# An attention kernel of eight batches: roundings of keys one unit later on ScalarE, values moved out of the key gaps, and a fifth buffer of probabilities

## What is computed

```python
x = x + _L0_xattn_ref(_layernorm(x), ctx, ...)   # q, k with rotary positions, scores + temporal bias, softmax, gate
x = x + _L0_ffn_ref(_layernorm(x), ...)          # three matrices and tanh
x = x + _L1_xattn_ref(_layernorm(x), ctx, ctx, mask, ...)
x = x + _L1_ffn_ref(_layernorm(x), ...)          # 8 experts, the best 2 weighted
# within an attention, per head:
scores = jnp.einsum('bhqd,bhkd->bhqk', q, k) * SCALE
attn = jax.nn.softmax(scores, axis=-1)
out = jnp.einsum('bhqk,bhkd->bhqd', attn, v)
```

## Time and profile before

| | before |
|---|---|
| median of 3 runs | 566.13 us (564.79 to 567.99) |
| the profiled execution | 565.75 us, its span 564.2 us |
| TensorE busy | 508.7 us (90%) |
| ScalarE busy | 434.1 us (77%) |
| VectorE, GpSimd busy | 278.4 and 168.3 us |
| exponentials, 416 in all | 1.03 us each |
| batch 0, 1, 2 end about at | 119, 187, 255 us |
| batches 4 to 7 | 54 to 56 us each |

### The profile page before, as it was taken

One profiled execution on the slowest core, in us unless ns is written; L12 is line 12 of the kernel. 1 busy time (PEld: TensorE's weight loads), 2 busy tenths in 40 slices (PEclk: granted clock), 3 DMA queues, 4 the chain that ended last, 5 costly groups with the idle time before them and its releaser, 6 DMA issues.

```text
span 564.2 us, 15361 instructions
## 1 busy us (share of the span) xinstructions
PE 508.7 (90%) x6338; PEld 260.1 (46%) x6338; DVE 278.4 (49%) x739; ACT 434.1 (77%) x496; POOL 168.3 (30%) x202
## 2 busy tenths in 40 slices
PE   7779898989889898899999999999999999998995
PEld 4434545445345544454555444444443443443344
DVE  5866556864785446553523252326343623450254
ACT  1265577777668787887988999899989988999832
POOL 4476817485685306840001001100000000000000
PEclk9788999999999999999999999999999999999996
DMA  8586965398568513671464383149112920000000
GB/s 270 157 264 207 292 214 151 130 291 264 131 189 271 168 43 95 220 231 52 96 146 146 95 167 93 60 106 230 57 37 69 222 75 7 7 1 2 6 6 16
DMA packets 51584, 74.53 MB, mean 132 GB/s; under 512 B 11146, under 2 KB 40050, under 8 KB 51506
## 3 DMA queue, kind: packets, MB, share of 16 engines
q1 hardware_dynamic: 40258, 37.54, 26.4%
q0 software_dynamic: 5632, 24.07, 12.7%
q10 hardware_dynamic: 5616, 11.86, 6.6%
HBM read 39.95 MB, written 18.83 MB: 104 GB/s over the span
## 4 chain that ended last, share of the span: by engine, by line
PE 59%; ACT 14%; issue 10%; DVE 8%; POOL 5%; DMA 3%; ACTq 1%; DVEq 0%
PE ps L539 26%; PE ps L515 16%; ACT probs L1167 9%; PE ps L450 3%; PE ps L440 2%; PE ps L669 2%; ACT ctx_turned L1167 1%; DVE k_swapped L1476 1%; PE ps L444 1%; ACT ctx_tokens L1167 1%; DMA k_scratch<-k_parts 1%; ACT k_parts L1192 1%; PE ps L551 1%; ACT ctx_normed L1167 1%; DMA wvg_columns<-in_wvg_columns 1%
## 5 line engine op out<-in xcount | busy, mean ns | idle before, releaser
L1167 ACT ACTIVATE probs<-ps 124x1024 f32<-124x1024 f32 (+1 forms) x305 | 296.3, 1025 | 53.1 <-PE ps L520 41.7
L515 PE MATMUL ps<-q_side,k_side 64*124 64x256 bf16 (+1 forms) x1664 | 162.0, 290 | 35.3 <-ACT probs L1167 26.6
L539 PE MATMUL ps<-probs,values 124*9 124x256 f32 (+1 forms) x2440 | 162.8, 382 | 0.0
L515 PEld LDWEIGHTS ps<-q_side,k_side 64*124 64x124 bf16 (+1 forms) x1664 | 79.6, 131 | 142.0 <-ACT probs L1167 74.7
L539 PEld LDWEIGHTS ps<-probs,values 124*9 124x9 f32 (+1 forms) x2440 | 52.8, 90 | 64.6 <-issue 17.4
L1051 POOL TENSOR_TENSOR post_rstd<-post_rstd,power 128x2 f32<-128x2 f32 x12 | 8.5, 712 | 194.0 <-DVE post_rstd L1691 126.5
L520 PE MATMUL ps<-bias_near,bias_w 64*124 64x84 bf16 (+1 forms) x416 | 42.2, 200 | 0.0
L1167 ACT ACTIVATE ctx_tokens<-ps 124x1024 f32<-124x1024 f32 (+1 forms) x37 | 38.0, 1026 | 5.0 <-PE ps L515 4.0
L1476 DVE SCALAR_TENSOR_TENSOR k_swapped<-ps,beta_products,k_table_sb 32x496 f32<-32x496 f32 (+2 forms) x64 | 40.4, 632 | 0.9
L1167 ACT ACTIVATE ctx_turned<-ps 124x1024 f32<-124x1024 f32 (+1 forms) x37 | 37.9, 1025 | 3.4 <-PE ps L515 2.4
L1167 ACT ACTIVATE ctx_normed<-ps 124x1024 f32<-124x1024 f32 (+1 forms) x37 | 37.9, 1026 | 2.4 <-PE ps L515 1.6
(11 more groups left out here) (256 smaller groups left out, 633.3 us busy)
## 6 DMA issues: line engine op xcount, KB each, us to landing
k_side<-k_scratch SPq DMA_DIRECT2D x24, 400.2 KB, 8.1
k_scratch<-k_parts POOLq DMA_DIRECT2D x16, 372.0 KB, 4.9
k_side<-k_parts SPq DMA_DIRECT2D x45, 124.0 KB, 2.4
q_side<-q_parts SPq DMA_DIRECT2D x63, 64.0 KB, 2.4
v_scratch<-values POOLq DMA_DIRECT2D x4, 936.0 KB, 8.8
values<-v_scratch SPq DMA_DIRECT2D x4, 936.0 KB, 13.9
v_scratch<-v POOLq DMA_DIRECT2D x12, 288.0 KB, 5.0
mask_q<-in_mask POOLq DMA_DIRECT2D x8, 400.5 KB, 4.5
```

What stands on the lines that cost most here:

```text
L515: last = pe.matmul(ps[0:width, bank, SQ * i:SQ * (i + 1)], kst[rows, j % 2, 2 * g + i, at], qst[rows, query_slot(j, run), 2 * g + i, :], s ...
L539: last = pe.matmul(ps[32 * i:32 * i + VC, ACC + g // 2, SQ * (g % 2):SQ * (g % 2) + SQ], v[0:rows, j % 2, t, h, :], probs_of(u)[0:rows, SQ ...
L1167: act.activation(probs_of(u)[0:rows, :], ps[0:rows, s:s + 2, :].rearrange("p a n -> p (a n)"), ACT.Exp)\
```

## The change

Six things are changed. ScalarE's roundings of layer 1's keys come 3 and 7 units behind the key step, where it was 2 and 6. In batches 1 and 2 `values_at` gives no unit of values in the pair whose even slot begins a key step, and four in the pair after it. For that to be possible in batch 2, its steps move from slots 7, 11, 18, 25 to 8, 12, 18, 26. There is a fifth buffer of probabilities, used from batch 1 on (so eight buffers from batch 3 on). The memory for it comes from `num` and `q_table`, which now lie in it; both are used only in batch 0. And `store_keys(0, 0)` is split: the stores of the keys go before `second_parts(1)`, that of the values stays behind it.

```diff
-        first = {at: (j + 1, n) for n, at in enumerate((10, 14, 20, 26) if j == 1 else (7, 11, 18, 25))}
+        first = {at: (j + 1, n) for n, at in enumerate((10, 14, 20, 26) if j == 1 else (8, 12, 18, 26))}
...
     if j < WIDE_FROM:
-        return 2
+        key_pairs = [] if j == 0 else [at // 2 for at in range(2 * VALUES_FULL) if keys_at(j, at) is not None and keys_at(j, at)[2] == 0]
+        return 0 if pair in key_pairs else 4 if pair - 1 in key_pairs else 2
...
-            return u % 4 if u < WIDE_FROM * UB else (u - WIDE_FROM * UB) % 7
+            return u % 4 if u < UB else (u - UB) % 5 if u < WIDE_FROM * UB else (u - WIDE_FROM * UB) % 8
...
-        num, den, inside = sb("num", [128, SQ]), sb("den", [128, SQ]), sb("inside", [128, SQ], BF16)
+        num, den, inside = p_fifth[:, 2 * SQ:3 * SQ], sb("den", [128, SQ]), sb("inside", [128, SQ], BF16)
...
             low_parts(1)
+            store_keys(0, 0, "k")
             second_parts(1)
-            store_keys(0, 0)
+            store_keys(0, 0, "v")
...
-                for lag, part in ((2, second_keys), (6, middle_of_second)):
+                for lag, part in ((3, second_keys), (7, middle_of_second)):
```

More of the change, by code:

```diff
@@ L190, in main_path @@
         near = sb("bias_near", [128, KT, NEAR], BF16)
[L191 removed]
+        p, p_fifth = sb("probs", [128, 4, HG * SQ]), sb("probs_fifth", [128, HG * SQ])
         def prob_slot(u):
[L195 removed]
+            return u % 4 if u < UB else (u - UB) % 5 if u < WIDE_FROM * UB else (u - WIDE_FROM * UB) % 8
         def probs_of(u):
             slot = prob_slot(u)
[L200 removed]
+            return p[:, slot, :] if slot < 4 else (p_fifth[:], ct[:], cn[:], tok[:].rearrange("p t d -> p (t d)"))[slot - 4][:, 0:HG * SQ]
         def taken_ahead(u):
@@ L246, in main_path @@
         rab = sb("x_rstd", [128, XT, 2])
-        q_table = sb("q_table_sb", [128, 2, SQ])
+        q_table = p_fifth[:, 0:2 * SQ].rearrange("p (i n) -> p i n", n=SQ)
         q_cos, q_sin = q_table[:, 0, :], q_table[:, 1, :]
@@ L1271, in scalar_program @@
             act.dma_start(G["centre_ident"][:], G["centre_ident_in"]).then_inc(ident_in, 16)
-            act.dma_start(q_table[:], G["q_table"]).then_inc(q_tab_in, 16)
+            act.dma_start(q_table, G["q_table"]).then_inc(q_tab_in, 16)
             act.dma_start(wvg_columns[:], G["wvg_columns"]).then_inc(beta_in, 16)
```

34 lines of the change are left out of this document (18 added, 16 removed).

## The result

| | before | after |
|---|---|---|
| median | 565.46 us (4 runs, 563.68 to 567.99) | 560.0 us (4 runs, 558.98 to 560.27) |
| ratio, with its interval | | 0.990 (0.9877 to 0.9923) |
| the profiled execution, its span | 565.75 us, 564.2 us | 560.2 us, 558.6 us |
| first exponential of the loop starts | 29.87 us | 31.09 us |
| TensorE's idle time before score matmuls in 58 to 255 us, nearly all of it for exponentials | 15.3 us | 5.6 us |

The account below looks back on a forecast made before the run. TensorE, waiting for ScalarE's exponentials, was taken as the bound. Head 3.7, rest of batch 0 1.33, batch 1 0.92, batch 2 2.0, narrow steps -0.1 sum to 7.85 us: forecast 558.3 us, range 551.5 to 563.

Parts of the forecast that it names:

- What bounds the kernel: Batches making keys, 58 to 255 us: TensorE's 15.3 us of score waits for ScalarE's exponentials fall to about 6.
- The later roundings: Key-step gaps: the second exponential runs in ScalarE's 1.19 us of idleness; costs nothing, removes TensorE's 1.14 us wait.
- The sum for batch 2: Batch 2's four gaps: 0 for the first two, 0.9 for the third, 0.65 + 0.44 for the last; 2.0 us.
- No values in the gap, four units after it: Batches 1 and 2: same matmuls in another order, values covering ScalarE's rounding and next two exponentials; no cost outside narrow steps.
- the narrow step: Chunk 0, 124 keys: 0.4 us lost in batch 1, 0.3 won in batch 0; together -0.1, between -0.9 and +0.8.
- Batch 1: Gaps of batch 1: the first ones worth 0 because VectorE and GpSimd limit them; only the last gap's 0.92 us kept.
- The 1.14 us: Batch 1, before chunk 2's keys: the time won turns into TensorE waiting for VectorE, worth 0.
- The head: Start of batch 0: loop starts 1.1 to 1.4 us later, stall and slow stretch go; 3.7 us won, bounds 1.9 to 5.1.
- VectorE's chain moves up by 1.9 us: Batch 0's head: token load ends at 47.7, so k_swapped of chunk 3 comes 1.9 us earlier; 2.4 taken for TensorE's matmuls.
- The second term, 1.3: Batch 0's head: TensorE's 1.32 us wait at 60.60 goes, as ScalarE has one more exponential before it waits for GpSimd.
- the clock takes the head: Rival: idle before unit 2 and before 55 us drops the clock again, costing about the head's 3.7; 562 us, chance 0.15.
- Slower, by the middle rounding: Rival: GpSimd's L1029 waits for the later middle rounding, lengthening nine wide chunks, 9.2 us less 3.7; 571.6 us, chance 0.05.

Follow-up runs that it names:

- experiment 1: Kernel before with one edit: ScalarE's roundings of layer 1's keys 3 and 7 units behind the key step; ratio 0.993 to the kernel before.
- experiment 9: Kernel before with lags of 3 and 7 and batch 2's key steps at even slots 8, 12, 18, 26; 559.7 us, ratio 0.990.
- experiment 7: Changed kernel with two units of values in every pair of batches 1 and 2 again; 557.37 us, ratio 0.986 to the kernel before.
- experiment 4: Changed kernel with the roundings' lags back at 2 and 6; ratio 1.011 to the kernel before.
- experiment 2: Kernel before with lags of 3 and 7 and the stores of chunk 0's keys moved ahead of the second roundings; ratio 0.994.
- experiment 3: Changed kernel with the stores of chunk 0's keys back behind the second roundings of chunk 1; 558.85 us, ratio 0.989 to the kernel before.
- experiment 5: Changed kernel with the next batch's token load issued behind unit 2 instead of unit 6; 557.14 us, ratio 0.986 to the kernel before.
- experiment 6: Changed kernel with the middle rounding 6 units behind the key step instead of 7; 555.69 us, ratio 0.983 to the kernel before.
- experiment 10: Changed kernel with the token load behind unit 2 and the middle rounding 6 units behind; 558.67 us, ratio 0.988 to the kernel before.
- experiment 8: Changed kernel with matmuls on zeros in two of TensorE's waits in batch 0's head; 559.24 us, ratio 0.990 to the kernel before.
- experiment 11: Changed kernel with early token load, middle rounding at 6 and the stores of chunk 0's keys back as before; 559.03 us, ratio 0.986.
- experiment 12: Changed kernel with early token load, middle rounding at 6, stores as before and two units of values everywhere; 558.23 us, ratio 0.987.

## Why the prediction was right, and which step was mis-sized

*What bounds the kernel.* Right: TensorE's idle time before score matmuls in the three batches went from 15.3 to 5.6 us (about 6 was forecast), and the gaps kept what the chain behind them allowed.

*The later roundings.* Right as a mechanism, and it is the edit that carries the change in batches 0 and 1 (1.9 and 1.0 us with the lag alone). Wrong that it costs nothing wherever the step stands: with the odd slots of batch 2 it lost 1.4 us there, most of it at the lower clock behind a wait that had grown by 0.4 us. I had taken the new slots of batch 2 as a condition for the order of the values. They are a condition for the lag, worth 4.2 us (experiments 1 and 9). The sum for batch 2 came out right because both were in the change.

*No values in the gap, four units after it.* I took it as neutral but for the narrow step. It costs 0.6 us in batch 2 (experiments 7 and 9 against the changed kernel), within the bounds given for the narrow steps. What I did not see is that without the lag batches 1 and 2 lose 11.8 us with it, 5.4 of them to the lower clock (experiment 4).

*Batch 1.* The 1.14 us did turn into a wait for VectorE: 2.06 us until 148.41. The 0.92 us came out at 0.98. It is not safe, though: in experiments 1, 2, 3, 5, 6, 7 and 10 TensorE stood 0.6 to 1.2 us at the batch's end for the load of the far queries, and experiments 2, 3 and 5 kept 0.1, 0.1 and -0.1 us of it. The sum had no term for the clock here either, and the wait for VectorE brought a slow stretch (148.9 us). TensorE's waits for v and k_swapped from 58 to 255 us grew by 3.7 us, from 2.1 to 5.8, a little less than the 4 to 5 that were forecast.

*The head.* Here the sum failed: 3.7 forecast, 1.08 measured. The start was 1.22 us later, as reckoned (GpSimd's second rounding of chunk 1 began at 29.21 instead of 27.88, behind the two stores), and the stall went. The failing step is "VectorE's chain moves up by 1.9 us". It rests on the load of the tokens ending at 47.7. I said that its issue hangs on unit 6, whose scores come no earlier, and left out that with a start 1.2 us later the issue also comes later: 39.9, not 38.8. And I took its 8.9 us for a fixed price. The runs show 7.6 to 12.7 us for this load issued at 38.8 to 40.0. The row statistics moved up by 0.46 us, and the matmuls behind k_swapped, which had stood 0.69 us in their queue, by 1.15, where the sum had 2.4. The second term, 1.3, was right: at the full clock the stretch behind them takes 3.80 us (experiment 8), and it took 5.32 before, 1.52 more. And the sum had no term for the clock, which took 1.58 of it back: 1.15 + 1.52 - 1.58 = 1.09, against 1.08 measured.

*The clock.* The rival "the clock takes the head", with a chance of 0.15, was in good part what happened, and at the places that it named: 1.66 us of idle before unit 2 and 2.71 before 56.60, each followed by a slow stretch. The sign that the prediction named for it, a clock of 0.50 between 28 and 60 us, was met. Only the second stretch cost the head anything, 1.6 us. The rival left nothing of the head where the execution kept 1.1, so 562 was too high and 558.3 too low; 560.0 lies between the two and in the range. The gaps gave 5.1 us where the sum had 4.15, and so covered a part of what the head fell short; that is luck and not reckoning.

*Slower, by the middle rounding.* Did not occur: in a wide chunk GpSimd's last difference of layer 1's keys waited for nothing.

```profile
148.76 1.13 POOL L1031 TENSOR_TENSOR k_parts<-k,k_parts 128x496 bf16<-128x496 f32 x1
```

That the middle rounding should have been moved the other way in relation to the next chunk, I had in hand: the prediction names the 2.91 us that GpSimd waits for it, and that it comes right behind the next chunk's first rounding. I used it to limit the gain and didn't see that one unit less would free it.

*What stays open.* The head's share in the medians is read from one trace per kernel and from the mean clock of the other executions. Whether the clock alone holds experiments 10 to 12 back in those was not seen in a trace. What brings the clock down in one execution and not in another is open too. A kernel with a lag of 6 everywhere but in chunk 3 of batch 0, and with the early load, should have both gains; it was not run.

## What to carry to other kernels

An instruction put later on an engine must be judged by what it then stands in front of: here the same lag took away a wait of 0.9 us behind an even slot and made one 0.4 us longer behind an odd one, and the same rounding freed GpSimd's chain when it moved past another rounding and stopped TensorE when it stood before an exponential. A wait that grows by 0.4 us can cost more than 0.4 if TensorE's clock falls behind it, so read the granted clock beside every wait. Where a stall goes, look at what is late next and whether its duration is a price or a draw: a load in a crowded stretch is a draw, so issue it before the crowd. And of a change with many parts, run the parts: two of six carried this one, and the order of the values made it slower than before when the later lag was taken away.

## What the runs showed of the hardware

The same load of the tokens took 4.5 to 6.4 us when it was issued at 31.3 to 34.0 us, and 7.6 to 12.7 us when it was issued at 38.8 to 40.0, with the DMA engines' share at 1.03 to 1.07 over 40 to 44 us in the changed kernel. The Trainium skill (DMA: Bandwidth & Descriptors, Queues, rings and completion order) says that each DMA engine takes turns between the queue rows that have work, packet by packet; a load that is longer when others are under way agrees with that, and the wide spread at one place is more than I expected.

TensorE's clock fell to 0.50 behind waits of 1.66 us (the last spread) and 2.02 us (experiment 10), and not behind waits of 1.01 and 1.29 us (experiment 5, at 54.74 and 59.90). In experiment 3 a wait of 1.48 us at 39.99 left it at 1.00. But in experiments 1, 6 and 9 it fell at 27 us behind two waits close together, 1.03 and 1.02 us until 27.16 in experiment 1, while 0.54 and 1.03 us until 26.76 in the kernel before left it at 1.00. So in these traces the length of the last wait alone does not tell when it falls. By experiment 8 the slow stretch at 56.8 us cost the changed kernel 1.6 us, beside the 2.71 us of the wait before it, and the one at 32.9 us nothing that reached unit 18.
